# Product stage: VectorE takes over the copy of the transposed outer products; sheaf: the extraction by destination moves into the scan by source

## The chip, the cores and the metric

One Trainium2 chip, one of its cores. The metric is the device time of one execution in microseconds (us). The core has TensorE (PE in the profile: matmuls and transposes; PEld are its weight loads), VectorE (DVE), ScalarE (ACT), GpSimd (POOL) and SyncE (SP), and 16 DMA engines. An indirect DMA (a gather or a scatter by a list of row numbers) is issued by GpSimd.

## The reference, cut

Four graph layers run one after another on 12500 nodes and 400000 edges sorted by destination, each with a residual and a layer norm. The first two are not touched here. The other two (d = 16, x of 12500 x 16):

```python
# sheaf layer: messages along each edge, summed by source and by destination
F_s = householder(reflection(xs, xd)); F_d = householder(reflection(xd, xs))
L_sd = -jnp.einsum('eki,ekj->eij', F_s, F_d)
msg_s = coef[:, None] * jnp.einsum('eij,ej->ei', L_sd, xd)
msg_d = coef[:, None] * jnp.einsum('eji,ej->ei', L_sd, xs)
out = x - jnp.zeros_like(x).at[src].add(msg_s) - jnp.zeros_like(x).at[dst].add(msg_d)
return jax.nn.relu(out)

# product layer: row = src, col = dst
x_j = node_features[col]
m = jnp.einsum('ei,ej,ijh->eh', x_j, edge_attr_e3nn, W_msg_tp) * norm_msg_tp
m = jax.nn.silu(m)
m = m @ W_msg_lin * norm_lin
agg = jax.ops.segment_sum(m, row, num_segments=n_nodes)
```

## The kernel before, in words

The edges lie in 128 lanes of 3125, cut into 25 chunks of 125 columns (CH), a chunk into 25 groups of 5 columns (NG, GRP). A chunk is numbered i; the code of an even chunk, of an odd one and of the last stand apart (over_chunks), since their buffers alternate. Each engine has its own program; they meet in semaphores, and what waits on an engine holds up all that stands behind it there.

**Product stage** (product_edges, tiles pe_...). Per chunk VectorE masks the loaded rows X and runs 16 scans over them (L668), which spreads x of the destination over its edges. Then for each group q: VectorE multiplies X and A to an outer product of 128 x 640 (L1747); TensorE transposes it in five matmuls into pT in PSUM (L1775); ScalarE copies pT to outT in SBUF (L1809); TensorE multiplies outT by the weights (L1782) into pM; ScalarE applies Silu to pM and writes the messages M (L1811). There is one buffer each of outer, pT, outT and pM.

The first 20 columns of a chunk (DC) are summed by source through TensorE: from the sixth group on, each of 20 groups carries one such column. For it VectorE writes two one-hot tiles (ped_ohl, ped_ohh, L1324, L1326) and the wide product y or p_agg of 128 x 1600 (L1329), and TensorE adds it to ped_acc with four matmuls, eight records (L1314). On TensorE the order is transposes (T), sums, product matmul.

The other 105 columns (SC) are written to memory by GpSimd, one indirect DMA each (L1139), in the order by source. It waits for each five of them by the count of written message groups, and for the first five of a chunk until the first five groups of the chunk have their messages. A chunk's M is freed (mfree) when its scatters have landed; ScalarE waits for that two chunks later. After the last chunk src_order_scan reads the rows back and scans them by source.

**Sheaf stage.** sheaf_edges computes both messages and writes the scan by destination to a table in memory, scan16. lane_carries (sc) mends what crosses lanes. extract (sx) then gathers for each of 100 node columns the row at the end of its run (100 indirect DMAs on GpSimd, L427, in four rounds of 25 through staging tiles) and VectorE multiplies each round by a mask (L442). After some small blocks (sf, si, sm), src_order_scan (ss) scans the messages by source: SyncE loads a chunk, VectorE makes the keep mask and runs 16 scans (L1684), SyncE stores it to scan16. Then come lane_carries (sq) and extract (sw) by source. A block ends with all engines meeting.

## Time and profile before

| | |
|---|---|
| median of 3 runs | 38449.33 us |
| lowest, highest | 38229.62, 38707.31 us |
| the profiled execution | 38408.23 us |
| its span | 38406.5 us |
| mean granted clock of TensorE | 0.628 |
| busy, share of the span | PE 37%, PEld 28%, DVE 42%, ACT 7%, POOL 58% |
| scatters of the product stage (POOL, L1139) | 2625, 3131.6 us |
| table loads of ScalarE there (L1809 and L1811) | 300 and 300, 384.9 us each |
| extraction by destination (sx) | 32762.6 to 32894.0 us |
| scan by source of the sheaf (ss) | 32937.4 to 33116.4 us |
| product_edges, first outer product to last scatter | 33486.7 to 37745.8 us |

Times inside the profile count from the span's start. In the timeline a row is one or more equal instructions that follow each other: start, duration, engine, line, what it writes and reads, how many; in brackets how long its engine was idle ahead of it, and on whom it waited. TensorE's ends are modelled. The granted clock is 0.5 or 1.0 of TensorE's full 2.4 GHz.

### The profile page before, as it was taken

The numbers are of one execution on the slowest core, as the hardware profiler recorded it, in microseconds if no ns is written. First come the engines' busy times: TensorE is split into PE (matmuls) and PEld (weight loads), VectorE is DVE, ScalarE is ACT, GpSimd is POOL, SyncE is SP. The second block draws the span as 40 slices with busy tenths as digits, with TensorE's granted clock in tenths as the row PEclk, the third lists the DMA queues.
The fourth block names the chain that finished last, engine by engine and source line by source line (L and its number), as shares of the span: only waits on it lengthen the run. The fifth ranks groups of instructions, "written<-read, shape, count | busy, mean of one in ns | idle before, by whom it ended". The sixth has DMA issues, their size and how long they took to land. (4 is left out here: it accounts for less than half of the span.)

```text
span 38406.5 us, 266237 instructions
## 1 busy us (share of the span) xinstructions
PE 14357.5 (37%) x71326; PEld 10765.9 (28%) x71326; DVE 16060.9 (42%) x34560; ACT 2592.4 (7%) x3901; POOL 22432.8 (58%) x20450
## 2 busy tenths in 40 slices
PE   1111110111111047665566613433434344166664
PEld 1110000101010036554455612222223222044443
DVE  2332237223232546774566713332333344244443
ACT  0000000000000000000000000100101000033330
POOL 5777761355555256663676645755675665477773
PEclk5555555555555567776787856666666666577775
DMA  2011113111111311111111110000000000200001
GB/s 45 13 13 12 12 12 115 24 19 21 19 21 19 102 37 28 29 29 18 25 30 29 28 9 11 10 12 9 10 12 9 10 12 9 54 15 15 13 15 48
DMA packets 1089229, 935.10 MB, mean 24 GB/s; under 512 B 580668, under 2 KB 1031892, under 8 KB 1063892
## 3 DMA queue, kind: packets, MB, share of 16 engines
q1 hardware_dynamic: 440100, 695.25, 6.2%
q0 software_dynamic: 646368, 201.76, 6.1%
q10 hardware_dynamic: 1872, 28.29, 0.2%
q8 instruction: 307, 5.03, 0.1%
q14 instruction: 582, 4.77, 0.0%
HBM read 497.08 MB, written 426.83 MB: 24 GB/s over the span
## 5 line engine op out<-in xcount | busy, mean ns | idle before, releaser
L1139 POOL DMA_INDIRECT messages<-se_M,se_rstage x2625 | 3090.6, 1177 | 2987.9 <-DVE se_M L1502 2193.8
L1139 POOL DMA_INDIRECT messages<-pe_M,pe_rstage x2625 | 3131.6, 1193 | 1098.1 <-issue 791.8
L495 POOL DMA_INDIRECT g1g_G<-tab,g1g_stage x3125 | 3036.7, 972 | 1039.9 <-issue 1028.2
L495 POOL DMA_INDIRECT se_G<-tab,se_stage x3125 | 3036.6, 972 | 1039.9 <-issue 1026.2
L495 POOL DMA_INDIRECT g2g_G<-tab,g2g_stage x3125 | 2954.1, 945 | 1039.9 <-issue 1020.9
L495 POOL DMA_INDIRECT c1c_G<-tab,c1c_stage x2125 | 2473.0, 1164 | 658.9 <-issue 640.8
L495 POOL DMA_INDIRECT c2c_G<-tab16b,c2c_stage x2125 | 2457.1, 1156 | 658.9 <-issue 641.5
L1038 DVE SCALAR_TENSOR_TENSOR g2gh_junk<-g2gh_pB,g2gh_src_f,earlier 128x128 f32<-128x128 f32 (+4 forms) x2625 | 1459.0, 614 | 2804.2 <-remote 2136.7
L1447 DVE TENSOR_TENSOR se_V<-se_pTV,s_b 128x160 f32 (+1 forms) x625 | 202.8, 324 | 5740.6 <-remote 3207.6
L737 PE MATMUL g1gh_acc<-g1gh_oh_hi,g1gh_oh_lo 128*128 128x100 bf16 x6250 | 770.9, 272 | 4595.6 <-issue 3480.3
L1536 PE MATMUL se_pTV<-ident,se_pair 128*32 128x128 f32 x3125 | 585.9, 333 | 4058.2 <-DVE se_pair L1443 2428.0
L715 DVE TENSOR_TENSOR g1gh_oh_lo<-dst_lo,iota 128x640 bf16<-128x640 f32 (+1 forms) x625 | 511.3, 818 | 3658.4 <-remote 2892.4
L1050 PE MATMUL g2gh_pB<-ident_b,src_lo 128*128 128x128 bf16 x2625 | 653.2, 282 | 3477.5 <-issue 2425.5
L1253 PE MATMUL c2cm_acc<-c2cm_hot,c2cm_part 128*128 128x512 f32 x6500 | 1744.8, 428 | 412.9 <-DVE c2cm_hot L1244 281.0
L1253 PE MATMUL c1cm_acc<-c1cm_hot,c1cm_part 128*128 128x512 f32 x6500 | 1745.5, 428 | 398.1 <-DVE c1cm_hot L1244 372.7
L737 PEld LDWEIGHTS g1gh_acc<-g1gh_oh_hi,g1gh_oh_lo 128*128 128x128 bf16 x6250 | 539.0, 133 | 4827.5 <-issue 3686.9
L1550 PE MATMUL se_pTV<-s_w,se_hid 128*128 128x32 f32 x6250 | 960.9, 308 | 1885.6 <-issue 1024.1
L1550 PEld LDWEIGHTS se_pTV<-s_w,se_hid 128*128 128x128 f32 x6250 | 964.6, 232 | 2129.4 <-issue 1338.4
L1536 PEld LDWEIGHTS se_pTV<-ident,se_pair 128*32 128x32 f32 x3125 | 300.4, 111 | 4475.6 <-issue 4410.8
L1253 PEld LDWEIGHTS c2cm_acc<-c2cm_hot,c2cm_part 128*128 128x128 f32 x6500 | 1350.5, 212 | 719.8 <-issue 420.1
L1253 PEld LDWEIGHTS c1cm_acc<-c1cm_hot,c1cm_part 128*128 128x128 f32 x6500 | 1351.3, 212 | 702.2 <-issue 400.7
L1747 DVE TENSOR_TENSOR pe_outer<-pe_X,pe_A 128x640 f32 x625 | 521.4, 834 | 2255.4 <-DMA g1w_X<-spread_buf 917.4
(614 smaller groups left out, 34863.2 us busy)
## 6 DMA issues: line engine op xcount, KB each, us to landing
scans<-g1w_W SPq DMA_DIRECT2D x25, 3187.5 KB, 9.9
c1cm_row<-match SPq DMA_DIRECT2D x500, 128.0 KB
c2cm_row<-match SPq DMA_DIRECT2D x500, 128.0 KB
edges<-g2g_G SPq DMA_DIRECT2D x25, 2062.5 KB, 6.4
g2w_G<-edges SPq DMA_DIRECT2D x25, 2062.5 KB, 11.6
scans<-g2w_W SPq DMA_DIRECT2D x25, 2062.5 KB, 7.3
g1g_G<-tab,g1g_stage POOLq DMA_INDIRECT x3125
g2g_G<-tab,g2g_stage POOLq DMA_INDIRECT x3125
```

Of the source, the lines that this page charges most:

```text
L495: g.indirect_dma_start(out=G[b][:, t, :], out_offset=None, in_=table, in_offset=bass.IndirectOffsetOnAxis(ap=stage[b][:, t:t + 1], axis=0) ...
L715: v.tensor_tensor(oh_lo[o][b][:, part, :], bc(lo[:, at], [P, m, P], 2), bc(k.iota[:, :], [P, m, P], 1), ALU.is_equal).then_inc(ready, 1)
L737: mm = pe.matmul(acc[2 if o and direct else o][:, 0:NT], oh_lo[o][b][:, g, :], oh_hi[o][b][:, g, :], start=False, stop=True, skip_group_ch ...
L1038: ins = v.scalar_tensor_tensor(out=junk[g][:, :], in0=pB[b][:, a * GRP * P:(e + 1) * P], scalar=src_f[:, e:e + 1], in1=k.earlier[:, (GRP - ...
L1050: pe.matmul(pB[b][:, e * P:(e + 1) * P], k.src_lo[:, at].to_broadcast([P, P]), k.ident_b[:, :], start=True, stop=False)
L1139: g.indirect_dma_start(out=view, in_=M[b][:, DC + t, :], in_offset=None, out_offset=bass.IndirectOffsetOnAxis(ap=stage[b][:, t:t + 1], axis=0)
L1253: mm = pe.matmul(self.acc[m % 2][:, :], self.part[part][:, j * MR:(j + 1) * MR, :].rearrange("p r f -> p (r f)"), self.hot[m % 2][:, j, :] ...
L1447: v.tensor_tensor(V[:, bass.ds(q * GRP, GRP), :, :].rearrange("p c n d -> p c (n d)"), pV[:, 0:GRP * 2 * D].rearrange("p (c n) -> p c n", ...
L1536: mm = pe.transpose(pT[:, g * P:(g + 1) * P], pair[:, g, :, :].rearrange("p n d -> p (n d)"), k.ident[:, :])
L1550: mm = pe.matmul(pV[:, g * 2 * D:(g + 1) * 2 * D], flat[:, g * P:(g + 1) * P], w2[:, :], start=True, stop=True)
L1747: v.tensor_tensor(outer[:, :, :, :], bc(X[b][:, at, :], [P, GRP, D, DE], 3), bc(A[b][:, at, :], [P, GRP, D, DE], 2), ALU.mult).then_inc(ou ...
```

## The change

In the product stage the copy of pT to outT goes from ScalarE to VectorE: for each group but a chunk's first, VectorE first waits for the transposes of the group before, copies them, and then makes its outer product; the last group's copy stands at the chunk's end. ScalarE keeps Silu alone. TensorE's product matmul now also waits for the Silu of the group before it (silued), which begins one higher; the counts at which GpSimd and VectorE wait rise by one to fit. In the sheaf stage sheaf_edges and lane_carries use a table of their own, by_dst_scans; the block sx is gone, and src_order_scan (ss) gets a program for GpSimd: 100 gathers straight into agg by the tile order["end"], without staging, and one mask product on VectorE behind the scans.

```diff
@@ scatter_column_loop
-            g.wait_ge(ready, i + 1 if parts == 1 else i * NG + (DG + t // GRP + 1))
+            g.wait_ge(ready, i + 1 if parts == 1 else i * NG + (DG + t // GRP + 2))
@@ src_order_scan
+        if ends:
+            order, end_scans, end_values = ends
+            taken, masked = c.pool_dma_sem(name + "_taken"), c.sem(name + "_masked")
...
+            if ends:
+                @block.gpsimd
+                def _(g):
+                    for t in range(NT):
+                        g.indirect_dma_start(out=end_values[:, t, :], out_offset=None, in_=end_scans[0:E, :],
+                                             in_offset=bass.IndirectOffsetOnAxis(ap=order["end"][:, t:t + 1], axis=0)
+                                             ).then_inc(taken, 16)
...
                 over_chunks(v, chunk, ch, D + extra)
+                if ends:
+                    v.wait_ge(taken, 16 * NT)
+                    v.tensor_tensor(end_values[:, :, :], end_values[:, :, :], bc(order["some"][:, :], [P, NT, D], 2),
+                                    ALU.mult).then_inc(masked, 1)
+                    v.wait_ge(masked, 1)
@@ product_edges, VectorE
-                    def outer_products(q):
+                    def copy_turned():
+                        v.tensor_copy(outT[:, :], pT[:, 0:GRP * P]).then_inc(copied, 1)
+
+                    def outer_products(q, first=False):
                         at = bass.ds(q * GRP, GRP)
                         v.wait_ge(transposed, i * NG + q + 1)
+                        if not first:
+                            copy_turned()
                         v.tensor_tensor(outer[:, :, :, :], bc(X[b][:, at, :], [P, GRP, D, DE], 3),
                                         bc(A[b][:, at, :], [P, GRP, D, DE], 2), ALU.mult).then_inc(outered, 1)
                     v.nop(nofuse=True)
-                    with v.Fori(0, DG + 1) as q:
+                    outer_products(0, True)
+                    with v.Fori(1, DG + 1) as q:
                         outer_products(q)
-                    v.wait_ge(silued, i * NG + DG)
+                    v.wait_ge(silued, i * NG + (DG + 1))
...
+                    v.wait_ge(transposed, i * NG + (NG + 1))
+                    copy_turned()
                     v.wait_ge(sums.made, (i + 1) * (2 * DC))
@@ product_edges, TensorE
                     pe.wait_ge(copied, n + 1)
+                    pe.wait_ge(silued, n + 1)
@@ product_edges, ScalarE
+                a.sem_inc(silued, 1)
...
-                        a.wait_ge(transposed, n + 2)
-                        a.activation(outT[:, :], pT[:, 0:GRP * P], ACT.Copy).then_inc(copied, 1)
                         a.wait_ge(product, n + 1)
@@ sheaf
+    by_dst_scans = k.dram("by_dst_scans", [E + P, D])
-        sheaf_edges(k, "se", tab, scan16, messages, first, carry,
+        sheaf_edges(k, "se", tab, by_dst_scans, messages, first, carry,
...
-        lane_carries(k, "sc", carry[:, 0:D], D, k.by_dst, ALU.add, scan16)
-        extract(k, "sx", scan16, k.by_dst, agg, D, ALU.add)
+        lane_carries(k, "sc", carry[:, 0:D], D, k.by_dst, ALU.add, by_dst_scans)
...
-        src_order_scan(k, "ss", messages, scan16, carry, D + 1, True)
+        src_order_scan(k, "ss", messages, scan16, carry, D + 1, True, (k.by_dst, by_dst_scans, agg))
```

The loop over two groups of 20 as VectorE has it, before (in the product stage, half of the loop; ISA rows are waits and address registers):

```order
L1747 ISA
L1747 REGISTER_ALU
L1747 TENSOR_TENSOR pe_outer<-pe_X,pe_A 128x640
L1323 ISA
L1324 ISA
L1324 TENSOR_TENSOR ped_ohl<-iota,src_lo 128x128
L1326 REGISTER_ALU
L1326 TENSOR_TENSOR ped_ohh<-iota,src_hi 128x100
L1328 REGISTER_ALU
L1329 ISA
L1329 TENSOR_TENSOR y<-ped_ohh,pe_M 128x1600
```

and the same half of the loop after the change:

```order
L1761 COPY pe_outT<-pe_pT 128x640
L1768 ISA
L1768 REGISTER_ALU
L1768 TENSOR_TENSOR pe_outer<-pe_X,pe_A 128x640
L1323 ISA
L1324 ISA
L1324 TENSOR_TENSOR ped_ohl<-iota,src_lo 128x128
L1326 REGISTER_ALU
L1326 TENSOR_TENSOR ped_ohh<-iota,src_hi 128x100
L1328 REGISTER_ALU
L1329 ISA
L1329 TENSOR_TENSOR y<-ped_ohh,pe_M 128x1600
```

The copy of the group before now stands ahead of the outer product; the order of the rest is kept. ScalarE's loop over the 25 groups of an even chunk, before:

```order
L1809 ACT_TABLE_LOAD
L1809 ACTIVATE pe_outT<-pe_pT 128x640
L1810 REGISTER_ALU
L1811 ISA
L1811 ACT_TABLE_LOAD
L1811 ACTIVATE pe_M<-pe_pM 128x80
L1806 REGISTER_ALU
L1806 COMPARE_AND_BRANCH
```

and after it:

```order
L1836 ISA
L1836 ACT_TABLE_LOAD
L1836 ACTIVATE pe_M<-pe_pM 128x80
L1833 REGISTER_ALU
L1833 COMPARE_AND_BRANCH
```

The copy and its table load are gone; the load ahead of Silu stays inside this loop. The loops of odd chunks and of the last one have no load, before or after. On GpSimd, between the lane carries by destination and those by source, the difference is

```order
-L423 COPY sx_si<-by_dst_end 128x25
-L427 DMA sx_gs<-scan,sx_si 128x16 x25
-L430 REGISTER_ALU
-L430 COMPARE_AND_BRANCH
-L418 UNCONDITIONAL_BRANCH
-L411 ISA x2
 L389 UNCONDITIONAL_BRANCH
 L391 DMA sm_row<-sm_tab,s_first_src 128x3
 L388 UNCONDITIONAL_BRANCH
 L374 ISA
+L1670 UNCONDITIONAL_BRANCH
+L1673 DMA s_agg<-by_dst_scans,by_dst_end 128x16 x100
```

so the gathers have moved behind the small gather of the block sm, into the block ss.

## Rows read from the trace of the kernel before

**Rows 1.** Table by stretches: busy us and count of each engine, clock, DMA share, GB/s.
```profile
33518.60:33686.80 168.20, 109.32 (x535) 77.17 (x534) 72.66 (x102) 74.04 (x91) 125.99 (x107) 0.79 0.05 14
```
**Rows 2.** Groups by line, product stage: busy us, mean ns | idle before, releasers.
```profile
L1139 POOL DMA_INDIRECT messages<-pe_M,pe_rstage x2625 | 3131.6, 1193 | 1098.1 <-issue 791.8 <-ACT pe_M L1811 306.3
```
**Rows 3.** Timeline, one group of an odd chunk: start us, us, engine, line.
```profile
34100.01 0.74 PE L1775 MATMUL pe_pT<-ident,pe_outer 128*128 128x128 f32 x5
34100.59 2.85 PE L1314 MATMUL ped_acc<-p_agg,ped_ohl 128*128 128x400 f32 x8
...
34101.00 0.82 DVE L1747 TENSOR_TENSOR pe_outer<-pe_X,pe_A 128x640 f32 x1 [1.07 <-PE pe_pT L1775]
...
34102.35 1.82 DVE L1329 TENSOR_TENSOR y<-ped_ohh,pe_M 128x1600 f32<-128x1600 f32 x1
...
34103.28 1.18 PE L1782 MATMUL pe_pM<-p_wm,pe_outT 128*128 128x16 f32 x10
...
34104.31 0.74 PE L1775 MATMUL pe_pT<-ident,pe_outer 128*128 128x128 f32 x5
...
34105.31 0.88 DVE L1747 TENSOR_TENSOR pe_outer<-pe_X,pe_A 128x640 f32 x1 [1.13 <-PE pe_pT L1775]
```
**Rows 4.** Timeline, the scatters of the same stretch on GpSimd.
```profile
34101.08 1.60 POOL L1139 DMA_INDIRECT messages<-pe_M,pe_rstage  x1 [0.31 <-issue]
...
34102.98 2.04 POOL L1139 DMA_INDIRECT messages<-pe_M,pe_rstage  x1 [0.30 <-issue]
...
34105.33 0.96 POOL L1139 DMA_INDIRECT messages<-pe_M,pe_rstage  x1 [0.30 <-issue]
```
**Rows 5.** Timeline, a group of an even chunk: ScalarE and GpSimd.
```profile
33527.55 1.28 ACT L1811 ACT_TABLE_LOAD   x1 [1.46 <-PE pe_pM L1782]
...
33530.25 2.04 POOL L1139 DMA_INDIRECT messages<-pe_M,pe_rstage  x1 [0.30 <-issue]
...
33535.25 2.05 POOL L1139 DMA_INDIRECT messages<-pe_M,pe_rstage  x1 [0.30 <-issue]
```
**Rows 6.** VectorE reading PSUM: two groups by line, then a timeline.
```profile
L177 DVE COPY g_h<-g1b_pO 128x480 f32 (+1 forms) x20 | 13.1, 657 | 51.5 <-PE g1b_pO L213 51.5
...
L1339 DVE COPY p_direct<-ped_acc 128x400 f32<-128x400 f32 x4 | 2.0, 566 | 3.6 <-PE ped_acc L1314 3.6
...
13949.96 0.88 DVE L1087 TENSOR_SCALAR c1ch_loT<-c1ch_pB,part 128x640 f32<-128x640 f32 x1
13950.46 0.94 POOL L495 DMA_INDIRECT c1c_G<-tab,c1c_stage  x1 [0.30 <-issue]
```
**Rows 7.** Timeline, ends and beginnings of chunks: TensorE, ScalarE, GpSimd.
```profile
33640.79 1.31 PE L1775 MATMUL pe_pT<-ident,pe_outer 128*128 128x128 f32 x5
...
33673.57 0.70 ACT L1809 ACTIVATE pe_outT<-pe_pT 128x640 f32<-128x640 f32 x1 [13.65 <-DMA g1w_X<-spread_buf]
...
33675.01 0.97 POOL L1139 DMA_INDIRECT messages<-pe_M,pe_rstage  x1 [0.30 <-issue]
...
33686.76 0.98 POOL L1139 DMA_INDIRECT messages<-pe_M,pe_rstage  x1 [8.73 <-ACT pe_M L1811]
...
33841.61 0.97 POOL L1139 DMA_INDIRECT messages<-pe_M,pe_rstage  x1 [0.30 <-issue]
...
33857.30 1.02 POOL L1139 DMA_INDIRECT messages<-pe_M,pe_rstage  x1 [12.69 <-ACT pe_M L1811]
...
34014.68 0.96 POOL L1139 DMA_INDIRECT messages<-pe_M,pe_rstage  x1 [0.30 <-issue]
```
**Rows 8.** Table by stretches, sheaf: extraction by destination, then scan by source.
```profile
32762.60:32894.00 131.40, 0.00 (x0) 0.00 (x0) 2.30 (x4) 0.00 (x0) 95.36 (x104) 0.50 0.09 6
...
32937.40:33116.40 179.00, 0.00 (x0) 0.00 (x0) 157.67 (x503) 0.00 (x0) 0.00 (x0) 0.50 0.68 248
```
**Rows 9.** Timeline, scans of a product chunk beside a scatter.
```profile
34112.00 6.03 DVE L668 TENSOR_TENSOR_SCAN pe_X<-keep_d,first,pe_X 128x125 f32<-128x125 f32 x16
...
34114.39 1.13 POOL L1139 DMA_INDIRECT messages<-pe_M,pe_rstage  x1 [0.31 <-issue]
```

More of the change, by code:

```diff
@@ L1618, in _, with src_order_scan @@
                 s.wait_ge(stored, 16 * (NCH + 1))
-def src_order_scan(k, name, messages, scans, carry, F, find_keep):
+def src_order_scan(k, name, messages, scans, carry, F, find_keep, ends=None):
     with ExitStack() as st:
```

## The prediction

> **What bounds the kernel now.** The page's first part comes first, and only to be put aside: its shares are means over the whole span, no engine's is near one, and the two stages that change must be read one by one.
>
> The product stage is read in the table by stretches, cut where the scatters of a chunk begin [rows 1]: such a period takes 168.2 us, and GpSimd is busy for 126 of it, more than any other engine. The groups by line say that its 2625 scatters cost 3131.6 us, with 791.8 us of gaps of 0.30 us between them, and that it waits for ScalarE's messages (pe_M) for only 306.3 us [rows 2]. So this stage is GpSimd's: 105 scatters in 154.8 us (33686.76 to 33841.61) or 157.4 (33857.30 to 34014.68), then a wait [rows 7]. For the order inside a chunk I read the timeline. The waits and the chain that ended last show the last stage only, and are not used.
>
> What makes a scatter long is VectorE. Undisturbed one takes 0.97 us and the next begins 0.30 us later, 1.27 in all. One that begins inside the wide product (1.82 us, both inputs in SBUF) takes 2.04 us and ends 0.85 us after it [rows 3, 4]: it stands until that instruction ends. In chunks with an odd number TensorE has no pause (T, the transposes, to T 4.30 us) [rows 3], and the scatters keep step with every second group: 8.60 us hold five of them (three of 0.97 to 1.50, one of 1.60, one of 2.04), 2.5 a group. In even chunks ScalarE loads a table twice a group; the group takes 5.01 us and holds three scatters, one of 2.04 us and two of about 1.0, so that the long ones begin 5.00 us apart [rows 5].
>
> In the sheaf stage the extraction by destination stands alone: 131.4 us in which GpSimd is busy for 95 and VectorE for 2.3. The scan by source is as much alone: 179.0 us, VectorE busy for 157.7, GpSimd not at all, DMA at 0.68 [rows 8].
>
> **Sheaf.** Removed: the block of 131.4 us. Added: 100 gathers beside the scan, one vector multiply of 128x1600 (1.82 us, as the wide product of that size [rows 3]) behind it. Scans keep GpSimd waiting too: beside them a scatter takes 1.13 us instead of 0.97, and 16 scans still follow one another without a gap, 6.03 us [rows 9]. So 100 gathers take about 100 x (1.13 + 0.30) = 143 us, inside the 179. They add their DMA share, 0.09 of 131 us = 12 us, to queues that are 0.68 busy; I take 4 us, bounds 0 and 12. Sum: -131.4 + 1.8 + 4 = **-126 us**. Without the cover all is paid: 0.
>
> **Product, one group.** ScalarE's copy (0.70 us [rows 7]) goes. VectorE gets a copy of 128x640 from PSUM, never seen here: copies from PSUM take 0.566 us for 400 columns and 0.657 for 480 [rows 6], so 0.82 to 0.84 for 640. Bounds: ScalarE's 0.70 below, the 0.88 of a compare of 640 columns from PSUM above. I take 0.83. Does it stop GpSimd as the wide product does? A gather that begins 0.50 us into that compare takes 0.94 [rows 6], as long as gathers beside nothing. A source in PSUM leaves GpSimd alone, so the copy costs it nothing. The Trainium skill (SBUF — State Buffer, Who interferes with whom) speaks against this: it lists the copy among the instructions that can take the pair of ports shared with GpSimd. By that rule a scatter that begins in the copy would stand up to 0.83 us; but the same section exempts one that reads at most one operand from SBUF outside the two-port modes, and the trace agrees with the exemption.
>
> The loop through two groups [rows 3]: T starts, 0.95 later (0.99 for the outer product today, less one register instruction) the copy starts, 0.80 later the outer product, 3.17 later the wide product has ended (34101.00 to 34104.17), 0.13 later TensorE starts the sums; then 2.69 to the product matmul and 1.03 to the T of the group after next. 8.77 us for two groups: **4.385 a group**, against 4.30 for TensorE alone and 4.0 for VectorE alone. Odd chunks get slower by 0.085 a group, even ones faster by 0.63.
>
> **Product, scatters.** At 4.30 us a scatter that is released by one wide product reaches the next outer product within 0.08 us of its start (34105.33 against 34105.31 got in; 34101.08 against 34101.00 stood 0.6 us) [rows 3, 4]. That alternation gives 2.5 a group. Three a group need 3.81 us plus one stand. If the group is 0.05 longer, the first scatter is always ahead of the outer product, lying in the new copy, and three fit, as at 5.01. At 4.385 I expect **three scatters a group**: 60 in 87.7 us. The other 45, from an even chunk: 157.3 - 100.2 = 57.1. So 105 take 144.8 us: 12.5 less in 12 even chunks, 10.0 less in 13 others (the last chunk has no loads): **-280 us**.
>
> **Product, the wait ahead of a chunk's scatters.** The last scatter starts at 33675.01; the fifth message group is written only then, and the next scatter starts at 33686.76 [rows 7]: 11.75. Ahead of an even chunk it is 15.7 (33841.61 to 33857.30). Until the scatters are over, TensorE's results reach the others late, up to 30 us: transposes that start at 33640.79 and take 1.31 are copied at 33673.57 [rows 7]. All 24 waits behave so, the release following the end of the scatters by 6 to 7 us, so this does not shrink with faster engines. Behind the release, an even chunk has three table loads and a copy on the path. ScalarE keeps one load a group there (the order above), so it saves 2.0 us: 11 x 2.0 = -22. But with shorter scatters the next chunk's first groups have about 49 us beneath them instead of 54 to 62; I charge 1.5 us a chunk, +36. The first chunk has no scatters above it: five groups of about 4.5 instead of 6.05 us, one load still at the end: -6. VectorE now also copies a chunk's last group before it goes on to the next chunk, 0.83 us beneath the scatters: 0; without them it would be 25 x 0.83 = 21. Product: -280 - 22 + 36 - 6 = **-272 us**.
>
> The remaining load reselects the table that is in place. If it cost nothing rather than 1.28 [rows 5], 14 us more would go. The Trainium skill (ScalarE: Activation LUTs, Table sets: the hidden batching unit) has the copy in every set, so that alternation would need no loads; the trace disagrees with its 300 + 300 here, all in even chunks.
>
> **Sum.** 38408.2 - 126 - 272 = 38010. That execution lies 41 us below the median of the runs, 38449.3; on the median's scale 38050.
>
> **Rivals.**
> (1) GpSimd's alternation stays at 2.5 a group: TensorE hides the 0.085, or the copy is nearer 0.70. Then 105 scatters take 155.5 in every chunk (12 x 1.9 less, 13 x 0.7 more: -14), the stage gives 14 + 22 + 6 = 42 us, and the sum is 38449 - 126 - 42 = 38280. For it: 0.05 us decides.
> (2) The extraction is not hidden: late semaphores, as in rows 7, hold VectorE's and SyncE's hand-overs until the gathers are over. 38449 - 272 = 38180. Against it: scans beside scatters show no gap [rows 9].
> (3) The late results follow GpSimd's rate, and with three scatters a group the fifth group is ready in time. The 24 waits of 12 to 14 us shrink to 2: 38050 - 260 = 37790.
> (4) **Slower.** A group's results come late in the main part too, since TensorE now pauses in front of the sums with its transposes unreported. One microsecond late makes a group 5.4 us; 60 scatters take 108, a chunk 165, 8 and 10 more than before: +227, and with the rest 38449 - 126 + 227 - 22 - 6 = 38520. It decides from a group of 5.2 us on. Against it: even chunks already pause 0.4 us before the product matmul and keep 5.01 exactly.
> (5) No effect, gains lost in waits nobody sees here: 38400 to 38450.
>
> **How the numbers follow.** Forecast 0.46, (1) 0.2, (2) 0.1, (3) 0.13, (4) 0.06, (5) 0.05. The likeliest gives 38050. From 37790 to 38330 lie the forecast, (1), (2) and half of (3); bounds of copy and DMA price add some 40 us. A measurement tells about 2% from no change, here 770 us; only (3) with all its bounds could pass 37680, and (4) would need twice its lateness to pass 39218. So faster 0.02, same 0.96, slower 0.02.
>
> **What would show it.** VectorE's copy from pe_pT at 0.82 to 0.84 us; T to T at 4.36 to 4.42 in all chunks; scatters three a group and 143 to 147 us a chunk; waits ahead of chunks of 12 to 15 us; no extraction block between the sheaf's first lane carries and its scan, the scan at 180 to 195 us with 100 gathers in it. Wrong would be: a copy over 0.95, a scatter stretched by it, a mean scatter still near 1.19 us, or a scan above 210 us.

## The result, and the profile after

The changed kernel takes 38193.57 us (median of 21 runs) against 38565.05 for the kernel before (21 runs); the ratio is 0.9891, with a 95% interval of 0.9864 to 0.9917. Ratios here are taken from the fast runs alone, those within 1.5% of the fastest of their kernel (20 of the 21 before, 15 of the 21 after); the medians are of all runs, and their ratio is 0.9904. The profiled execution of the changed kernel spans 38090.6 us, that of the kernel before 38406.5.

So the time forecast, 38050, is 0.4% off. The working behind it is not right: neither stage did what its line of the sum says. In the profiles the two stages give 224 us, where the medians differ by 371; drawing the 21 and 21 times again at random puts that difference between 163 and 441 us, so the 147 us between the two are not established. I read the two traces stage by stage, each from its first to its last landmark:

| stage | before | after | difference | forecast |
|---|---|---|---|---|
| up to the sheaf's lane carries (nothing changed) | 32741.3 | 32650.4 | -91 | 0 |
| sheaf: lane carries to the product stage's first outer product | 745.4 | 682.0 | -63 | -126 |
| product: first outer product to last scatter | 4258.1 | 4097.6 | -161 | -272 |
| the rest | 661.7 | 660.7 | -1 | 0 |

The first landmark is one instruction in each trace (the line's own view; duration min/median/max in ns, then first and last start in us), before and after:

```profile
L348 POOL DMA_INDIRECT sc_ends<-scan,by_dst_mend_from x1: 982/982/982, 32741.3 to 32741.3; - x1
```
```profile
L348 POOL DMA_INDIRECT sc_ends<-by_dst_scans,by_dst_mend_from x1: 982/982/982, 32650.4 to 32650.4; - x1
```

Not one instruction ahead of it was changed, and it comes 91 us earlier. Two later executions, of kernels that are equal up to there, reach it at 34153.6 and at 34604.0 us on the same chip, 450 us apart. The stages without a change swing by more between two executions than the whole change is worth; only stage lengths, which repeat within a few us, can be compared in single profiles.

**The product stage after.** Groups by line, the scatters (busy us, mean ns, then idle time before them and what ended it), to be read against [rows 2]:

```profile
L1139 POOL DMA_INDIRECT messages<-pe_M,pe_rstage x2625 | 3189.5, 1215 | 853.8 <-issue 788.6 <-ACT pe_M L1836 54.8 <-POOL pe_rstage L1132 10.4
```

The forecast wanted shorter scatters; they became longer (3131.6 us before, 3189.5 after). The mean of 1.215 us and the scan below are two of the signs that the prediction itself named for being wrong. What went is the wait for ScalarE's messages: 306.3 us before, 54.8 after. Taken from first to last scatter start of each chunk and from there to the next chunk's first, the stage is 31.9 + 3899.9 + 326.3 = 4258 before, and 26.3 + 3956.9 + 114.4 = 4098 after: the start gives 6 (as forecast), the chunks cost 57, the waits give 212. The timeline of a chunk's end in the changed kernel, to be read against [rows 7]:

```profile
33866.61 0.97 POOL L1139 DMA_INDIRECT messages<-pe_M,pe_rstage  x1 [0.30 <-issue]
33869.00 0.27 POOL L1132 COPY pe_rstage<-rank 128x105 int32 x1 [1.42 <-DMA messages<-pe_M,pe_rstage]
...
33870.15 0.99 POOL L1139 DMA_INDIRECT messages<-pe_M,pe_rstage  x1 [0.88 <-POOL pe_rstage L1132]
```

From the last scatter to the next chunk's first it is 3.5 us (6.1 ahead of an even chunk) instead of 11.8 (15.7), and it is GpSimd's own copy of the destinations that is waited for, not a message. The first messages of a chunk are now ready before the scatters of the chunk ahead of it end, and what holds them back is the two message buffers. The waits of the stage by engine (us in total, times, longest us) say the same: first a line of before, then two of after.

```profile
DVE pe_outer L1747 <- DMA g1w_X<-spread_buf: 917.4, 46, 36.3
```
```profile
DVE pe_outT L1761 <- PE pe_pT L1799: 1474.2, 604, 52.2
...
PE pe_pM L1807 <- ACT pe_M L1836: 988.7, 22, 50.3
```

In the kernel before, VectorE waited 46 times, up to 36 us, with a releaser named that had been done long ago (a DMA of an earlier stage): these are the results that come late. The changed kernel has no such line in this stage; its long waits begin with TensorE's, 22 of up to 50.3 us for ScalarE, which itself waits for a message buffer.

**A group after.** Timeline of an even chunk, which before had the table loads (start us, us, engine, line), TensorE's transposes, VectorE's three long instructions and the scatters:

```profile
34069.51 1.82 DVE L1329 TENSOR_TENSOR p_agg<-ped_ohh,pe_M 128x1600 f32<-128x1600 f32 x1
...
34070.68 1.50 POOL L1139 DMA_INDIRECT messages<-pe_M,pe_rstage  x1 [0.30 <-issue]
...
34070.92 0.74 PE L1799 MATMUL pe_pT<-ident,pe_outer 128*128 128x128 f32 x5
...
34071.69 0.82 DVE L1761 COPY pe_outT<-pe_pT 128x640 f32<-128x640 f32 x1 [0.36 <-PE pe_pT L1799]
34072.44 0.81 DVE L1768 TENSOR_TENSOR pe_outer<-pe_X,pe_A 128x640 f32 x1
34072.49 1.61 POOL L1139 DMA_INDIRECT messages<-pe_M,pe_rstage  x1 [0.30 <-issue]
...
34073.77 1.82 DVE L1329 TENSOR_TENSOR y<-ped_ohh,pe_M 128x1600 f32<-128x1600 f32 x1
...
34074.40 2.05 POOL L1139 DMA_INDIRECT messages<-pe_M,pe_rstage  x1 [0.30 <-issue]
...
34075.22 0.74 PE L1799 MATMUL pe_pT<-ident,pe_outer 128*128 128x128 f32 x5
```

The copy takes 0.82 us, as forecast, and it does not hold a scatter: 48 scatters begin inside a copy in this stage, and they take 0.965 to 0.984 us. Transposes to transposes is 4.30 us, not 4.385 (4.31 on average over such groups), and the scatter at 34072.49 begins 0.05 us inside the outer product and stands. The alternation of 2.5 scatters a group is the one of before.

**The sheaf stage after.** Table by stretches (VectorE's busy time is the third pair, GpSimd's the fifth, then clock, DMA share and GB/s): the whole scan by source with the gathers beside it, a piece of it in the middle of the gathers, a piece behind them.

```profile
32703.50:32964.00 260.50, 0.00 (x0) 0.00 (x0) 163.44 (x504) 0.00 (x0) 97.27 (x100) 0.50 0.50 174
...
32747.20:32831.20 84.00, 0.00 (x0) 0.00 (x0) 21.20 (x60) 0.00 (x0) 63.89 (x67) 0.50 0.24 70
32852.00:32953.40 101.40, 0.00 (x0) 0.00 (x0) 92.79 (x300) 0.00 (x0) 0.00 (x0) 0.50 0.72 264
```

The block of 131.4 us is gone, and the scan has grown from 179 to 260 us [rows 8]. Its work is what it was; beside the gathers VectorE is busy for a quarter of the time and the transfers fall from a share of 0.72 to 0.24. The timeline of VectorE shows how it waits:

```profile
32741.64 0.17 DVE L1698 COPY carry<-ss_O 128x16 f32<-128x16 f32 x1 [4.51 <-DMA c1cm_row<-match]
32742.80 0.16 DVE L1689 TENSOR_TENSOR keep_s<-ss_G,ss_prev 128x1 f32 x1 [0.99 <-DVE carry L1698]
32744.52 0.34 DVE L1690 TENSOR_TENSOR keep_s<-ss_G 128x104 f32 x1 [1.56 <-issue]
...
32768.22 0.17 DVE L1698 COPY carry<-ss_O 128x16 f32<-128x16 f32 x1 [8.69 <-issue]
```

Each of these instructions needs a result of VectorE itself, and the one ahead of it on that engine ended 1 to 9 us earlier; the releasers named in the brackets do not fit that. The gathers run unbroken from 32704.3 us on and the first hand-over that is late ends at 32741.64. A chunk of the scan takes some 7 us for the first three chunks, 28.0 us for three in the middle of the gathers, and 6.8 on average again once the last gather is over. This is rival (2): late hand-overs that hold as long as GpSimd's gathers follow one another.

### The profile page after: what moved, and what is told of

Same layout as the page of the kernel before. It is cut to its first block and busy times, and to the rows that moved or that the text cites. A ratio compares the mean times of both kernels' runs of the same rounds, so it can differ in the third digit from the quotient of the medians.

```text
span 38090.6 us, 265807 instructions
## 1 busy us (share of the span) xinstructions
PE 14262.1 (37%) x71326; PEld 10763.8 (28%) x71326; DVE 16527.8 (43%) x35182; ACT 1769.8 (5%) x2976; POOL 22573.8 (59%) x20446
## 5 line engine op out<-in xcount | busy, mean ns | idle before, releaser
L1139 POOL DMA_INDIRECT messages<-se_M,se_rstage x2625 | 3102.9, 1182 | 2958.4 <-DVE se_M L1502 2163.6
L1139 POOL DMA_INDIRECT messages<-pe_M,pe_rstage x2625 | 3189.5, 1215 | 853.8 <-issue 788.6
L1244 DVE TENSOR_SCALAR c2cm_hot<-c2cm_row,c2cm_first 128x512 fp32r<-128x512 f16 x3250 | 1312.5, 480 | 53.6 <-issue 50.9
```

Source lines behind the costliest of these rows:

```text
L1139: g.indirect_dma_start(out=view, in_=M[b][:, DC + t, :], in_offset=None, out_offset=bass.IndirectOffsetOnAxis(ap=stage[b][:, t:t + 1], axis=0)
L1244: v.tensor_scalar(self.hot[m % 2][:, j, :], self.row[:, 0, m * BE * P:(m + 1) * BE * P], self.first[:, j:j + 1], None, ALU.is_equal).then_ ...
```

## The experiments

**Two kinds of chips.** The experiments fell on four chips, and with the runs of the result they show two kinds. Where the kernel before takes 38.6 ms (the runs of the result), 40.4 (e8 to e10) or 40.7 ms (e11, e12), results come late beneath GpSimd's indirect transfers; where it takes 32.9 (e1 to e4) or 32.8 ms (e5 to e7), no wait of the product stage looks late. A line that no experiment touches tells them apart in a profile: in the sheaf's edge loop the scatters wait for VectorE's messages, here in the changed kernel on a chip of the first kind, then in a kernel with the same edge loop on one of the second.

```profile
L1139 POOL DMA_INDIRECT messages<-se_M,se_rstage x2625 | 3102.9, 1182 | 2958.4 <-DVE se_M L1502 2163.6 <-issue 794.0 <-POOL se_rstage L1132 0.8
```
```profile
L1139 POOL DMA_INDIRECT messages<-se_M,se_rstage x2625 | 3164.7, 1206 | 879.6 <-issue 792.5 <-DVE se_M L1502 67.9 <-POOL se_rstage L1132 19.2
```

A scatter costs nearly the same on both (1182 and 1206 ns); the wait is 2163.6 us on one and 67.9 on the other. The first kind is not one speed: that wait is 3185.2 us in e8 and 3553.5 in e12. Each of the four chips was met once, so nothing here tells a lasting trait of a chip from a condition of that hour. The ratios compare kernels on one chip, and all comparisons below are within a kind; but the kernel before was profiled on the chip of the result alone, so stage lengths are compared across chips where e8 to e12 are set against it. The changed kernel's stages repeat within 4 us from that chip to e8's. The stage lengths are those of the table above; "waits" is the sum from each chunk's last scatter start to the next one's first.

| kernel | kind | sheaf | product | mean scatter ns | waits | ratio to before (95%) |
|---|---|---|---|---|---|---|
| before | first | 745 | 4258 | 1193 | 326 | 1 |
| changed | first | 682 | 4098 | 1215 | 114 | 0.9891 (0.9864 to 0.9917) |
| e8 changed | first | 685 | 4100 | 1216 | 114 | 0.9970 (0.9922 to 1.0017) |
| e9 nudge | first | 682 | 4136 | 1170 | 263 | 0.9988 (0.9947 to 1.0028) |
| e10 outer product twice | first | 740 | 4152 | 1216 | 96 | one run, 40420 us against 40435 |
| e11 the kernel of e5 | first | 606 | 4530 | 987 | 507 | 1.0094 (1.0060 to 1.0129) |
| e12 gathers paced | first | 604 | 4104 | 1217 | 115 | 0.9937 (0.9897 to 0.9977) |
| e1 product part alone | second | 738 | 4069 | 1214 | 89 | 0.9993 (0.9984 to 1.0003) |
| e2 sheaf part alone | second | 601 | 4113 | 1219 | 116 | 0.9966 (0.9952 to 0.9980) |
| e3 gathers paced | second | 600 | 4095 | 1214 | 114 | 0.9963 (0.9948 to 0.9977) |
| e4 and one-hot rows in PSUM | second | 602 | 3773 | 1091 | 114 | 0.9864 (0.9848 to 0.9880) |
| e5 and attributes in PSUM | second | 602 | 3519 | 993 | 116 | 0.9782 (0.9766 to 0.9799) |
| e6 outer product twice | second | 738 | 4117 | 1229 | 92 | one run, 32866 us against 32809 |
| e7 gathers paced | second | 600 | 4094 | 1214 | 115 | one run, 32671 us against 32809 |

**Each part alone (e1, e2).** The first is the diff's lines in the scatter loop and in product_edges, the second those in src_order_scan and sheaf.

> The kernel before with the product part alone. In the profile of the changed kernel the product stage (first outer product to last scatter) went from 4258 to 4098 us, and stages that the change does not touch were together 91 us shorter, which no part of the change explains. Theory D (the two parts are separate, the 91 us are scatter between executions): product stage 4098 us within 5, the sheaf stage as before, the whole 38565 - 160 = 38405 us, ratio 0.996. Rival S (something of the product part, such as its program text or its place in memory, also shortens other stages): the unchanged stages are again some 90 us shorter, the whole near 38310.

> The kernel before with the sheaf part alone. Theory D: from the start of the sheaf's first lane carries to the first outer product of the product stage it saves 63 us as in the changed kernel, since the scan by source takes 255 us instead of 179 with 100 gathers in its first half; product stage 4258 us as before; the whole 38565 - 63 = 38500, ratio 0.998. Rival S: unchanged stages again 90 us shorter, 38410. A scan near 183 us here would say that the slow scan of the changed kernel was an accident of that execution.

Both fell on a chip of the second kind, where no result comes late, so their forecasts in us for the first kind were not put to the test. With the sheaf part alone, which leaves the product code as it was, the product stage takes 4113 us and the waits are 116, not 4258 and 326. With the product part added to that (e3 has both) it is 4095. So without late results the product part is worth 18 us, and 23 by its ratio of 0.9993, whose interval (-10 to 53 us) does not tell it from nothing. The sheaf part gives 138 us in its own stage (738 to 601), where the forecast had 126, and 112 by its ratio of 0.9966 (66 to 158).

The 26 us between 138 and 112 are within that interval, but the product stage has a place for them. With the sheaf part in the program, GpSimd's copy of the destinations ahead of every second chunk is 2.3 us late, whether the product code is the old or the new. GpSimd's waits for it in e1 (first line) and e2 (us in total, times, longest):

```profile
POOL pe_rstage L1132 <- DMA messages<-pe_M,pe_rstage: 37.4, 24, 1.8
```
```profile
POOL pe_rstage L1132 <- issue: 43.7, 11, 4.0
POOL pe_rstage L1132 <- DMA messages<-pe_M,pe_rstage: 18.4, 13, 1.4
```

The 11 waits for nothing that the profile shows stand where GpSimd's loop goes back to its start. That 100 more instructions of GpSimd ahead of it shift where this loop lies in the program is my guess; it was not tried. 138 less 26 is 112; that the ratio gives the same number is closer than its interval warrants.

Rival S would have given the product part 90 us more, a ratio of 0.997; e1's interval excludes it on the second kind; on the first kind, where the 91 us were seen, no run has the product part alone.

**The gathers paced (e3, e7, e12).** On top of the changed kernel:

```
                     for t in range(NT):
+                        if t and t % 4 == 0:
+                            g.wait_ge(scanned, t // 4 * 1)
                         g.indirect_dma_start(out=end_values[:, t, :], out_offset=None, in_=end_scans[0:E, :],
```

> The changed kernel, with the 100 gathers handed out four to a chunk of the scan: GpSimd waits for the scan's count of chunks in front of every fourth gather. Theory L (VectorE's own completions are reported late once gathers have followed one another without a pause for some 25 us; a pause keeps that away): no chunk of the scan is slowed, the scan takes 179 to 186 us instead of 255, the whole 70 us less than the changed kernel: 38193 - 70 = 38120. Rival P (each gather delays the scan by its own traffic or by the port it shares with VectorE, 76 us for 100 gathers, 0.76 us each): the scan stays near 255 us, spread evenly over its 25 chunks, and the time stays near 38190.

> The changed kernel with four gathers to a chunk of the scan, once more, since its first run fell on a chip of the second kind, where the scan was not slowed even unpaced (168.8 us). On a chip of the first kind theory L expects a scan of 170 to 186 us instead of the 255 of the changed kernel, rival P 255 us.

> The changed kernel with four gathers to a chunk of the scan. Both its runs so far fell on chips of the second kind, where the scan takes 168 us paced or not. On a chip of the first kind, where the unpaced scan took 249 to 251 us in three profiles, theory L expects 168 to 175 us and a sheaf stage (lane carries to first outer product) of 600 to 610 us instead of 682 to 685: gathers that come in fours with a pause of 1.5 us between never make a result late. Rival P (each gather costs the scan 0.8 us): 249 us. If 4 in 6.8 us is still too many, the scan lies between.

Twice this fell on the second kind, where the unpaced scan is as fast (first scan to end of the last 169 us in e2, 167 in e3), and told nothing. The third time it fell on the first kind, and there it decides. The stretch of the scan, to be read against the 260.50 us above:

```profile
35235.00:35414.00 179.00, 0.00 (x0) 0.00 (x0) 158.25 (x508) 0.00 (x0) 100.23 (x100) 0.50 0.71 253
```

and its timeline, with 16 scans in one piece again beside four gathers and a pause:

```profile
35249.34 5.36 DVE L1697 TENSOR_TENSOR_SCAN ss_O<-keep_s,carry,ss_G 128x105 f32<-128x105 f32 x16
35249.84 1.05 POOL L1675 DMA_INDIRECT s_agg<-by_dst_scans,by_dst_end  x1 [0.30 <-issue]
35251.19 1.01 POOL L1675 DMA_INDIRECT s_agg<-by_dst_scans,by_dst_end  x1 [0.31 <-issue]
35252.51 1.01 POOL L1675 DMA_INDIRECT s_agg<-by_dst_scans,by_dst_end  x1 [0.30 <-issue]
...
35255.18 0.94 POOL L1675 DMA_INDIRECT s_agg<-by_dst_scans,by_dst_end  x1 [1.66 <-DVE carry L1700]
```

The same 100 gathers now cost the scan nothing: 604 us for the sheaf stage against 682 and 685 in the three profiles without the pause, as theory L says, and rival P (each gather costs the scan 0.8 us) is out. Those three come from two other chips of the first kind; that e12's own chip makes results late is seen in its edge loop (3553.5 us) and in e11. A pause of 1.66 to 1.99 us after four gathers keeps the scan's results on time.

**Stands taken away (e4, e5, e11).** These start from the paced kernel of e3. A scatter "stands" where it waits inside its own time for VectorE's instruction to end. In e4 the one-hot rows of the wide product lie in PSUM, in e5 also the attributes that the outer product multiplies with:

```
-        sums = DirectSums(c, name + "d", wide)
+        pH = c.ps(name + "_pH", [P, 512])
+        sums = DirectSums(c, name + "d", wide, [pH[:, 0:NT], pH[:, 256:256 + NT]])
...
+                        v.wait_ge(outered, i * NG + q + 1)
+                        v.tensor_copy(pA[:, :, :], A[b][:, at, :]).then_inc(moved, 1)
+                        v.wait_ge(moved, i * NG + q + 1)
                         v.tensor_tensor(outer[:, :, :, :], bc(X[b][:, at, :], [P, GRP, D, DE], 3),
-                                        bc(A[b][:, at, :], [P, GRP, D, DE], 2), ALU.mult).then_inc(outered, 1)
+                                        bc(pA[:, :, :], [P, GRP, D, DE], 2), ALU.mult).then_inc(outered, 1)
```

> The paced kernel of the run before this one, and in the product stage the one-hot rows of the wide product (128x100, two of them) lie in PSUM instead of SBUF, so that the wide product has one operand in SBUF. Theory W (a scatter stands only for instructions with both operands in SBUF): the scatters of 2.04 us vanish, three scatters fit in a group of 4.31 us with one stand of 0.55, 105 scatters take about 143 us instead of 158.5, and the product stage loses 24 x 15 = 360 us: 38120 - 360 = 37760. Rival L2 (with fewer stands the scatters come nearer to following one another without a pause, and results are reported late in the main part too): groups longer than 5 us in places, 105 scatters still under 145 us but waits of 10 us and more ahead of chunks, 38000 or more. Rival U (the operand in PSUM changes nothing): 158 us, 38120.

> The kernel with the one-hot rows of the wide product in PSUM, and now the outer product too has one operand in PSUM: VectorE first copies the five edges' attributes of a group (40 values a partition) there. Then no instruction of a group has both operands in SBUF except two short comparisons. The runs so far fell on two chips: on one the kernel before took 38.5 ms and results came late beneath uninterrupted scatters, on the other 32.9 ms and none came late. Theory W (stands come only from instructions with two SBUF operands): 105 scatters take 134 to 138 us, nothing else on their path, so against the kernel with the rows alone in PSUM (143 us expected there) another 24 x 5 to 8 = 120 to 190 us go, on a chip of the second kind: 32300 us. Theory L on a chip of the first kind: GpSimd now never pauses inside a chunk, results come late everywhere, a chunk takes more than 180 us, the whole is above that of the kernel before. Rival V: the small copy and its two waits lengthen VectorE's part of a group beyond 5.2 us, scatters then wait for messages, 32500.

> The kernel with the one-hot rows and the attributes in PSUM once more. Its first run fell on a chip of the second kind (kernel before 32.8 ms, nothing late) and gave 0.9782. On a chip of the first kind (38 to 41 ms) theory L says that a kernel whose scatters never stand has results late in every group: the scatters of a chunk still take 135 us, but waits for messages of tens of us come between them, the product stage is at or above the 4100 us of the changed kernel and may pass the 4258 of the kernel before; against L would be a stage of 3519 us as on the other chip. On a chip of the second kind: ratio 0.978 again.

On the second kind theory W holds. Timeline of e4: a wide product of 1.82 us with a scatter inside it that takes 0.97, and the outer product, with both inputs still in SBUF, holding one at 1.45.

```profile
28832.80 0.81 DVE L1771 TENSOR_TENSOR pe_outer<-pe_X,pe_A 128x640 f32 x1
28833.00 1.45 POOL L1139 DMA_INDIRECT messages<-pe_M,pe_rstage  x1 [0.30 <-issue]
...
28834.14 1.82 DVE L1329 TENSOR_TENSOR y<-pe_pH,pe_M 128x1600 f32<-128x1600 f32 x1
28834.76 0.97 POOL L1139 DMA_INDIRECT messages<-pe_M,pe_rstage  x1 [0.31 <-issue]
28836.03 0.97 POOL L1139 DMA_INDIRECT messages<-pe_M,pe_rstage  x1 [0.30 <-issue]
```

The duration of VectorE's instruction is the same with one operand in PSUM, and three scatters fit in a group of 4.30 us. Most chunks take 145 to 146 us (expected 143), in e5 135 (expected 134 to 138), and the whole is 0.9864 and 0.9782 of the kernel before. The product stage lost 322 us in e4 (360 expected) and 254 more in e5 (120 to 190 expected). The Trainium skill (SBUF — State Buffer, Who interferes with whom) says that an instruction of VectorE with at most one input in SBUF, outside the two-port modes, does not contend with GpSimd. Here the trace agrees with it by intervention: same work, one operand moved, 2.05 becomes 0.97 us.

On the first kind the same kernel is slower than the kernel before, 1.0094 (1.0062 by the medians of all runs), although its sheaf stage is 139 us shorter. Its scatters, groups by line, and below them what waits longest in the product stage:

```profile
L1139 POOL DMA_INDIRECT messages<-pe_M,pe_rstage x2625 | 2589.7, 987 | 1886.0 <-ACT pe_M L1845 1128.5 <-issue 757.5
```
```profile
DVE pe_outT L1766 <- DMA g1c_ends<-scans,by_dst_mend_from: 1472.5, 289, 9.8
ACT pe_M L1845 <- DMA g1w_X<-spread_buf: 1236.2, 123, 12.7
```

The scatters are 600 us cheaper than in the changed kernel, and 1128.5 us of waiting for messages have come. VectorE waits 289 times with a releaser long done, that is, in every second group or so, and groups take 7.3 to 7.8 us on average in the main part instead of 4.4. One of them:

```profile
36549.42 0.74 PE L1808 MATMUL pe_pT<-ident,pe_outer 128*128 128x128 f32 x5
```
```profile
36554.15 0.82 DVE L1766 COPY pe_outT<-pe_pT 128x640 f32<-128x640 f32 x1 [4.91 <-DMA g1c_ends<-scans,by_dst_mend_from]
```

The transposes end at 36550.2, the copy that waits for them starts at 36554.15; in the changed kernel that step takes 0.03 us (34070.92 + 0.74 to 34071.69). Taking away what kept GpSimd standing has brought the late results into the main part, as L expected, and its bound for the stage held (4530, above 4258). Its picture of a chunk did not: the 105 scatters take 156 to 165 us, not 135, since they come in runs of mostly 15 with waits of 4 to 5 us between, and the waits ahead of chunks are 16 to 25 us. The late copy above lies 8 us into such a run. On the same chip e12, which has the stands, has a product stage of 4104 us. e4, with the wide product's stands alone taken away, was not run on a chip of this kind.

**Stands added (e6, e10).** In the kernel before, in the first five groups of each chunk only:

```
                         outer_products(q)
+                        v.wait_ge(junked, i * (DG + 1) + q + 1)
+                        v.tensor_tensor(junk[:, :, :, :], bc(X[b][:, at, :], [P, GRP, D, DE], 3),
+                                        bc(A[b][:, at, :], [P, GRP, D, DE], 2), ALU.mult).then_inc(junked, 1)
```

> The kernel before, and in the first five groups of each chunk VectorE makes the outer product a second time into a tile that nobody reads, so that each of these groups stops GpSimd once or twice for up to 0.8 us. On a chip of the first kind: theory L (results come late only beneath scatters that follow one another without a pause) expects these groups to take some 5 us each instead of up to 35, the first scatter of a chunk within 7 us of the last of the one ahead instead of 12 to 16, and 80 to 200 us less in the product stage in spite of 75 to 100 us of added stands. Rival R (the results come late since ScalarE, which waits for TensorE twice a group, is in the loop, and the cure of the change was to take it out of the first step): the waits stay at 12 to 16 us and the stage becomes longer than 4258 us. On a chip of the second kind no result is late before either and the stage is 0 to 60 us longer.

> The kernel before with the outer product of the first five groups of each chunk made twice, once more: on a chip of the second kind as the run before (some 55 us slower than the kernel before, no late result), on a chip of the first kind theory L expects the waits ahead of chunks to fall from 12 to 16 us to under 7.

e6 fell on the second kind, where nothing is late: product stage 4117 us, mean scatter 1229, waits 92. There is no profile of the kernel before from such a chip; e2 less the 26 us found above would be 4087, so the stands cost some 30 us by that estimate and 57 by the one run's time, and bring nothing. The expectation was 0 to 60. e10 on the first:

```profile
L1139 POOL DMA_INDIRECT messages<-pe_M,pe_rstage x2625 | 3192.6, 1216 | 927.7 <-issue 793.4 <-ACT pe_M L1818 124.0 <-POOL pe_rstage L1132 10.3
```

Work was added to VectorE, ScalarE still copies, and the stage is 106 us shorter than in the kernel before (4152 against 4258), with scatters 61 us dearer and the waits at 96 us instead of 326. The first message groups of chunk 1, ScalarE's timeline:

```profile
35745.86 0.24 ACT L1818 ACTIVATE pe_M<-pe_pM 128x80 f32 x1 [2.50 <-PE pe_pM L1789]
...
35763.27 0.24 ACT L1818 ACTIVATE pe_M<-pe_pM 128x80 f32 x1 [2.90 <-PE pe_pM L1789]
```

17.4 us from the first to the fifth; in the kernel before these lie 58.6 us apart, the copy at 33673.57 [rows 7] among them. The longest wait ahead of a chunk is 5.2 us (expected: under 7). Rival R, that ScalarE's place in the chain makes the lateness, is out: ScalarE is where it was. It is not a clean cure. In 9 of the 13 even chunks (counted from 0) the way from first to last wide product takes 169 to 205 us, against 96 undisturbed: late results moved into the main part, where the head start hides them. Nor does the one run of the whole show a gain, 40420 us against 40435.

**The changed kernel, and a small instruction more (e8, e9).**

```
                             copy_turned()
+                        v.wait_ge(junked, i * NG + q + 1)
+                        v.tensor_copy(junk[:, 0:128], aside[:, 0:128]).then_inc(junked, 1)
```

> The changed kernel itself, beside the kernel before on whatever chip this falls on. On a chip of the second kind (the kernel before at 32.8 to 32.9 ms) the two parts add up: 23 us for the product part and 112 for the sheaf part by the two runs with one part each, 44 and 138 by their stages in the profiles; theory D expects ratio 0.9950 (0.994 to 0.996). If the parts help or hinder each other it lies outside. On a chip of the first kind (38.5 ms) 0.9891 again.

> The changed kernel with one more small instruction of VectorE in every group, between the copy and the outer product: a copy of 128x128 from a PSUM bank of its own to a tile that nobody reads, about 0.2 us. The forecast held that three scatters fit into a group once the group is 0.05 us longer than 4.30, and the changed kernel then ran at 4.31 with 2.5 to 2.6 scatters a group, since a scatter that starts 1.15 us after the end of a wide product starts just inside the outer product (it begins 1.09 us after that end). Theory T (it is a matter of who starts first): the outer product now begins 1.29 us after that end, the scatter gets ahead of it, three scatters to a group of 4.31 to 4.42 us, 105 scatters in 144 to 148 us instead of 158.5, product stage 24 x 11 to 14 = 260 to 340 us shorter than in the changed kernel: an instruction added, and ratio 0.986 to 0.988. Rival N: more work on VectorE only makes things longer or leaves them, 0.995 to 0.998.

e8 repeats the stages of the changed kernel within 4 us (4100 and 685), and misses the 0.9891 expected for the first kind: 0.9970, with an interval that ends at 0.9922. The 224 us that the two stages give are 0.9945 here, inside it, and the medians of all runs give 0.9952.

e9 was to show that three scatters fit once the outer product starts later. A scatter at 36173.82 began 0.01 us behind the start of an outer product at 36173.81, took 0.97 us and got through; mean scatter 1170 ns instead of 1216, chunks 154 us instead of 158.5. But groups take 4.6 us or more on average, and the late results are back: VectorE waits 62 times, up to 36.1 us, with a releaser long done, and the waits ahead of odd and even chunks are 10.7 and 11.9 us in the median (3.5 to 16.4).

```profile
L1139 POOL DMA_INDIRECT messages<-pe_M,pe_rstage x2625 | 3070.8, 1170 | 1010.6 <-issue 791.4 <-ACT pe_M L1842 218.3 <-POOL pe_rstage L1132 0.9
```

Neither T nor N foresaw that: T's ratio of 0.986 to 0.988 is out, and N's 0.995 to 0.998 lies in the interval, but N says nothing of late results. T's count of three a group was not reached (2.7 to 2.95 in most chunks), and no run on the second kind tells what it would have been. For L it is a third witness, and it answers a rival to e10, that any added work of VectorE helps: 0.28 us of instruction moved the scatters out of the outer products of the first five groups (44 scatters of 0.987 us there in chunk 1, against 14 of 1.160 in the changed kernel), and these groups went from 20.5 to 63.0 us.

## Why the prediction was right in its number and wrong in its working

- **The group.** Forecast 4.385 us from a loop through VectorE; measured 4.31 in the steady part of a chunk. Two terms were too long. From transposes to copy I put 0.95, taken from the outer product's 0.99; it is 0.77 (34070.92 to 34071.69). From copy to outer product I put 0.80; it is 0.75. The loop of two groups is then 8.54 instead of 8.77 us, below TensorE's 8.60, and TensorE stays the bound. The text named 0.05 us as what decides; one of the terms was off by 0.18. This is rival (1).
- **Scatters a group.** "Three" was wrong, it is 2.5 to 2.6, and 105 scatters take 158.5 us, not 144.8, nor the 155.5 of rival (1): once the first five groups run on time, each of them, too, makes a scatter stand (mean 1.160 us there in chunk 1, 0.968 before). That term was -280 and is +57.
- **The waits.** "This does not shrink with faster engines" was the step that failed furthest: 326 to 114 us. I took the lateness for something that lasts until the scatters are over. By the runs, it needs transfers of GpSimd that follow one another without a stop. In the kernel before, scatters slipped past the outer products of the first groups (42 scatters of 0.968 us in chunk 1). In the changed kernel copy, outer product and transposes form a loop of 4.38 us in which one scatter in three stands for 0.55 us (three of 1.27 and one stand are 4.36), and nothing comes late. Rival (3) had the effect (waits shrink) and a price of -260 against -212, but for a wrong reason: the rate is no higher, GpSimd stands for a moment between. e10, e11 and e9 show the condition from both sides.
- **The sheaf.** The work of it was right: 138 us on the second kind against 126. On the kind on which it was forecast it is 63, since the gathers have no pause. I named late hand-overs as rival (2), which came true by half, and gave it 0.1, "scans beside scatters show no gap": those were four scatters with stands. The kernel's own late results beneath unbroken scatters [rows 7] were the nearer row, and I did not carry them over from one stage to the other. e12 gives the price back: 604 us.
- **The copy** at 0.82 us, and that it does not hold a scatter, were right; a table load a group is left in even chunks, and the steady groups take 4.30 to 4.32 us with it or without.
- **Sum.** Forecast -398; the two stages give -224; the medians differ by 371. That the total came out near the forecast is luck: the terms -280, +14 and -126 measured +57, -212 and -63, and their errors in part cancel. The remaining 147 us no changed stage shows. The profiles put 91 of them into stages without a change, whose swing between executions is larger than that; whether they are chance (224 lies inside the 163 to 441 us named at the start, but not inside the interval of the ratio) or the change does something to other stages on that chip, stays open. e8's interval (-315 to +69 us) does not decide it.

What also stays open is why results come late at all, why on some chips (or at some times) alone, and how long a run of transfers must be: in the sheaf stage the first late hand-over ends 37 us after the gathers begin, in e11 one is late 8 us into a run. The traces show when, not how.

## What to carry to other kernels

An unbroken run of indirect transfers from GpSimd can make other engines' hand-overs late (here TensorE's and VectorE's), on some chips by up to 36 us each. Before work is put beside such a run, look whether the trace has waits with a releaser that was long done, and if so try to hand the transfers out in small lots with a wait between; four at a time was enough here. And a kernel in which an engine now and then stands may owe its pace to that: e5 is 2.2% faster than the kernel before on one kind of chip and 0.9% slower on the other, so time such a change on both.

## What was not expected of the hardware

- The same kernel takes 32.8 to 32.9 ms on some chips and 38.6 to 40.7 ms on others, with the same duration of the instructions looked at (scatter 0.97 us undisturbed on both, copy 0.82).
- On the slower chips VectorE's own completions, too, reach VectorE 1 to 9 us late beside unbroken gathers; with a pause of 1.66 to 1.99 us after every fourth they do not (e12).
- One stand of 0.4 to 0.55 us in every third scatter went with results on time (the first groups of odd chunks in e10, the changed kernel).
- A wide product with one of its two operands in PSUM takes the same 1.82 us and leaves GpSimd alone; with both in SBUF a scatter in it takes 2.05 us instead of 0.97.
